# A planner's stage order and its scan density in a fused kernel of four vision layers

## What is computed

```python
# layers 0, 2, 3 (each of 8 images, 56*56 pixels, 128 channels in 4 groups, 9 points)
xp = x @ w_in + b_in
h = gelu(batch_norm(depthwise_conv3x3(x)))
offset, mask = h @ w_off + b_off, softmax(h @ w_msk + b_msk)
y = sum over 9 points of mask * bilinear_sample(xp, point + offset)   # 4 corners a point
x = x + gamma1 * layer_norm(y @ w_out + b_out)
x = x + gamma2 * layer_norm(gelu(x @ w_fc1 + b_fc1) @ w_fc2 + b_fc2)
# layer 1 (Di = 256 channels, N = 16 states, K = 4 directions, L = 3136)
xb = silu(depthwise_conv3x3(layer_norm(x) @ in_proj))
h = h * exp(dt_t * A) + (dt_t * u_t) * B_t      # a recurrence over L, for each k, d, n
y_t = sum over n of h * C_t
x = x + (layer_norm(y) * silu(z)) @ out_proj;  x = x + mlp(layer_norm(x))
```

## The kernel before, in words

| drain at the end of stage | next stage | rounds (full scan ticks among them) at 2.611 | at 2.656 | at 12 |
|---|---|---|---|---|
| 16, (0, 7) | (2, 5) | 23 (4) | 3 (3) | 0 |
| 20, (2, 6) | (3, 6) | 51 (51) | 53 (53) | 42 |
| 21, (3, 6) | (2, 7) | 4 (0) | 0 | 0 |
| 22, (2, 7) | (3, 7) | 42 (0) | 42 (0) | 42 |
| 23, the end | none | 22 (0) | 22 (0) | 22 |

## Time and profile before

### The profile page before, as it was taken

One profiled execution on the slowest core, in us unless ns is written; L12 is line 12 of the kernel. 1 busy time (PEld: TensorE's weight loads), 2 busy tenths in 40 slices (PEclk: granted clock), 3 DMA queues, 4 the chain that ended last, 5 costly groups with the idle time before them and its releaser, 6 DMA issues.

```text
span 30032.1 us, 287320 instructions
## 1 busy us (share of the span) xinstructions
PE 22752.8 (76%) x94224; PEld 14355.0 (48%) x94224; DVE 22824.8 (76%) x36140; ACT 12178.8 (41%) x21705; POOL 21870.4 (73%) x21172
## 2 busy tenths in 40 slices
PE   5588788787887888877887788777877787777444
PEld 4444455444554454444544454445544454445433
DVE  1289987989599868998788859997799968994212
ACT  1144444444444444444444435444444444443000
POOL 6777777777677777777677767776677767566767
PEclk7798889888888888888988888888888888888666
DMA  3212222221222222212222122212222222112221
GB/s 76 74 54 68 55 68 68 61 65 52 75 63 56 64 74 54 66 52 62 70 62 66 49 73 59 61 54 66 60 59 64 55 71 55 46 49 70 63 58 53
DMA packets 2410663, 1854.55 MB, mean 62 GB/s; under 512 B 1686547, under 2 KB 2045509, under 8 KB 2409165
## 3 DMA queue, kind: packets, MB, share of 16 engines
q0 software_dynamic: 677376, 1388.62, 17.3%
q1 hardware_dynamic: 1731788, 447.55, 6.7%
HBM read 1569.35 MB, written 265.21 MB: 61 GB/s over the span
## 4 chain that ended last, share of the span: by engine, by line
DVE 35%; PE 29%; POOL 14%; issue 12%; ACT 7%; DMA 1%; SPq 1%; DVEq 0%; ACTq 0%; POOLq 0%
POOL d_g L746 14%; DVE l_wk L1334 7%; DVE l_wk L1311 7%; PE d_p L1037 6%; PE l_acc L1019 5%; DVE l_wk L1328 5%; DVE d_g L1354 5%; PE d_pr L1185 3%; DVE l_wk L1313 2%; PE d_pr L1239 2%; ACT l_pm L797 2%; PE d_pr L1072 1%; PE d_pr L1051 1%; ACT L973 1%; PE d_pr L1232 1%
## 5 line engine op out<-in xcount | busy, mean ns | idle before, releaser
L746 POOL DMA_INDIRECT d_g<-table,d_idx x21168 | 21870.2, 1033 | 8119.0 <-issue 6395.7
L1037 PE MATMUL d_p<-d_g,c_ident 128*128 128x128 f32 x43200 | 6019.1, 303 | 2046.9 <-DVE d_g L1354 2043.0
L1019 PE MATMUL l_acc<-l_wk,c_ident 128*128 128x448 f32 x14336 | 7290.6, 638 | 331.5 <-DVE l_yx L1299 263.7
L1037 PEld LDWEIGHTS d_p<-d_g,c_ident 128*128 128x128 f32 x43200 | 5874.6, 218 | 3118.9 <-DVE d_g L1354 2149.0
L1324 DVE TENSOR_TENSOR l_wk<-l_wk,l_pb 128x896 f32<-128x896 f32 x3584 | 3814.9, 1064 | 1604.7 <-PE l_pb L988 1601.3
L797 ACT ACTIVATE l_pm<-l_wk,l_a 128x448 f32<-128x448 f32 x3584 | 2271.2, 634 | 6232.1 <-DVE l_wk L1311 6219.5
L1019 PEld LDWEIGHTS l_acc<-l_wk,c_ident 128*128 128x128 f32 x14336 | 3174.7, 223 | 2397.9 <-issue 2224.1
L1334 DVE TENSOR_TENSOR l_wk<-l_wk,l_pc 128x896 f32<-128x896 f32 x3584 | 3795.0, 1059 | 38.0 <-ACT l_carry L778 24.2
L1311 DVE TENSOR_TENSOR_SCAN l_wk<-l_pm,l_carry,l_wk 128x448 f32<-128x448 f32 x3072 | 3496.9, 1138 | 5.1 <-ACT l_pm L797 2.3
L1354 DVE TENSOR_TENSOR d_g<-d_g,d_wt 128x512 f32<-128x512 f32 x1281 | 812.6, 688 | 2291.6 <-DMA d_g<-table,d_idx 2291.3
L1328 DVE TENSOR_TENSOR_SCAN l_wk<-l_wk 128x224 f32<-128x224 f32 x3584 | 2421.3, 676 | 0.3
(11 more groups left out here) (180 smaller groups left out, 23765.5 us busy)
## 6 DMA issues: line engine op xcount, KB each, us to landing
d_g<-table,d_idx POOLq DMA_INDIRECT x21168
table<-d_pst SPq DMA_DIRECT2D x2376, 64.0 KB
hd<-d_hst SPq DMA_DIRECT2D x168, 224.0 KB
d_htc<-hd SPq DMA_DIRECT2D x144, 256.0 KB
d_xin<-mid SPq DMA_DIRECT2D x112, 224.0 KB
mid<-d_xo SPq DMA_DIRECT2D x192, 128.0 KB
d_xres<-mid SPq DMA_DIRECT2D x192, 128.0 KB
d_xin<-in_x SPq DMA_DIRECT2D x56, 224.0 KB
```

Source lines behind the costliest of these rows:

```text
L746: e.indirect_dma_start(out=m.g[Q % SLOTS][:, j, :], out_offset=None, in_=m.table[k % 2], in_offset=bass.IndirectOffsetOnAxis(ap=m.idx[G % ...
L1019: ins = e.matmul(m.acc[:, h, 0:448], m.ident[:, :], m.hb[x % 4][:, h, :], start=(n == 0), stop=(n == 15))
L1037: ins = e.matmul(m.p0[:, t % 2 * 128:t % 2 * 128 + 32 * w], m.ident[:, :], m.g[Q % SLOTS][:, w * p:w * p + w, 32 * r:32 * r + 32], start=( ...
```

## The change

Two places of the code are touched. In `stage_order` the stages (0, 6) and (3, 0) swap places (8 and 9), and so do (3, 6) and (2, 7) (21 and 22): the order then ends with (2, 6), (2, 7), (3, 6), (3, 7). In `schedule` the bisection allows no forced round beyond those that pace 12 has. No instruction of any engine is added or taken away by either: they are put in another order.

```diff
-        return [(0, 0), (0, 1), (0, 2), (0, 3), (0, 4), (2, 0), (0, 5), (2, 1), (3, 0), (0, 6), (2, 2), (3, 1), (2, 3),
-                (3, 2), (3, 3), (2, 4), (0, 7), (2, 5), (3, 4), (3, 5), (2, 6), (3, 6), (2, 7), (3, 7)]
+        return [(0, 0), (0, 1), (0, 2), (0, 3), (0, 4), (2, 0), (0, 5), (2, 1), (0, 6), (3, 0), (2, 2), (3, 1), (2, 3),
+                (3, 2), (3, 3), (2, 4), (0, 7), (2, 5), (3, 4), (3, 5), (2, 6), (2, 7), (3, 6), (3, 7)]
...
     free = Planner(n, high).forced
     for _ in range(10):
         mid = (low + high) / 2
-        if Planner(n, mid).forced <= free + 40:
+        if Planner(n, mid).forced <= free:
             high = mid
```

## The result

The changed kernel takes 30255.07 us (median of 4 runs, 30238.17 to 30270.23), against 30014.83 us for the kernel before, measured beside it (30010.79 to 30018.79). The ratio is 1.008 [1.0062, 1.0097]: slower by 240 us, where 690 us were forecast. The profiled execution took 30238.17 us, with a span of 30236.2 us and a mean granted clock of 0.845 (0.846 before). So its span is 204 us longer than that of before (30032.1 us), and this is the difference to take apart.

The account below looks back on a forecast made before the run. DVE's list was taken to bound the kernel while scans run, POOL without scans. - 349 + 1239 - 100 - 100 = + 690 us on 30034.1 us, less 16 us to the median, gave 30710 us; range 30000 to 31300 us (0.80).

Parts of the forecast that it names:

- The sign: Whole kernel: the change makes it slower, chance 0.81.
- DVE in the scan phase: While scans run: ticks cost DVE the same in all, 83 thirds fewer beside them at 4.2 us save 349 us.
- the upper bound of 5.8 us: Scan phase: most a third beside scans might cost, letting about 1.6 us of mixed-stage DVE idle time go with it.
- The pace: Scan ticks: pace rises from 2.611 to about 2.80, layer 1 ends at third 1538, 83 thirds earlier.
- The tail: After the scans: 83 more thirds where POOL alone sets the pace, at 14.93 us each, + 1239 us.
- A third beside scans: Scan phase: each third no longer beside scan ticks saves 4.2 us, bounds 3.13 and 5.8 us.
- The two drains beside scans: Before stages 21 and 17: removing them gains 100 us, not POOL's waits of 341.1 and 176.6 us; bounds 60 and 135.
- POOL is the bound throughout: Rival, whole kernel: POOL sets the time, its removed waits count in full, faster at 29440 or 29335 us; chance 0.12.
- Waits for B shrink: Rival, full and mixed stages: denser ticks halve DVE's waits, 500 to 700 us come back, 30000 to 30250 us; chance 0.10.
- The pace lands higher: Rival, scan ticks: at pace 2.95 they end 157 thirds earlier, + 1485 us, 31500 us; chance 0.08.

Follow-up runs that it names:

- e6_slack: Kernel before at its own pace 2.611, with layer 2 of images 1 to 4 a stage later in the order: 29860.75 us, ratio 0.9943.
- e8d_denser_apart: Changed kernel's order at pace 2.95, next stage's preparation held out of the transitions: 31039.28 us, 1.0334 of the kernel before.
- e1: Kernel before with the strict limit on forced rounds alone, order unchanged: 0.9832, 0.9871 and 0.9856 of the kernel before on three chips with standstills.
- e7_slack_apart: Kernel before at pace 2.611, layer 2 of images 1 to 4 a stage later, preparation held out of transitions: 29799.36 us, ratio 0.9926.
- e4b_before_apart: Kernel before at its own pace 2.611 and order, next stage's preparation held out of the transitions: 29806.19 us, ratio 0.9928.

## Why the prediction was wrong, and where it was right

**The sign was right, the size three times too large.** The step that failed is "DVE in the scan phase", in its first words: "The ticks cost it the same in all". I had read a full stage, found DVE's list full, and let that stand for the whole stretch of ticks. In the 3.5 ms of transitions PE sets the time, not DVE's list. Of the 337 us by which DVE idles in stage 19, 291 lie in the transition from 23983 to 24456 us (473 less 182.25). I had seen the idle time, and let a part of it go with the thirds (in the upper bound of 5.8 us), rather than ask which engine held the stage up and with what. The pace moves 89 preparation steps out of that regime, and with them PE's waits for inputs just written: a term of the sum that was missing altogether.

By the table above, the missing term is -535 us, and what it gave back beside the full ticks shows in the smaller saving there, -346 instead of -449. The two are -432 us of the -487 us between forecast and trace; the rest is the tail (-43) and the start (-12). At the 3.7 us a step that `e6_slack` measured, the 89 steps are 329 us; the other 100 of the 432 us are not shown to be the steps' alone, and 43 of them are the eighth transition's.

**The parts, one by one.**
- The pace: 2.802 and end third 1539, forecast 2.80 and 1538. Line 1479 ended at 26.71 ms, not 27.15, by what the transitions lost. It still lies in stage 20. Full stages took 1275 and 1292 us, not 1240 to 1280.
- The tail: 83 thirds at 14.98 us are 1243 us, less 147 for what went with them. Forecast +1139, measured +1096. Besides the 105.2 us before stage 23, POOL had waited 49.0 us for indices before stage 22, where the 4 rounds after stage 21 lie. In the changed kernel it waits for no indices after the scans. The prediction gave this second wait nothing, and it is about the 43 us by which the tail was missed. The tail is what makes the kernel slower.
- A third beside scans: 346 us for 74 thirds fewer there, 4.7 us with the drain before stage 21 in it and 3.3 with 100 us for the drains taken off, forecast 4.2. That it lies so near is luck: the 89 steps came in there, and at 2 us each (an estimate) the thirds and the drain saved 524 us, 7 us a third. The next 64 saved about 1 us each by the same reckoning (`e8d_denser_apart`). So there is no one price of a third.
- The two drains beside scans: POOL's 341.1 and 176.6 us went away, and the stretch of full ticks, which holds the longer of them, got shorter by 346 us with the thirds' saving in it. So they did not count in full beside the thirds. The 100 us given to them were not measured apart.
- *POOL is the bound throughout* fell: POOL's waits for buffers rose by 485 us and full stages by 70 to 90 us.
- *Waits for B shrink* named nearly the right time (30000 to 30250 us; the span is 30236), and the wrong cause. The waits for B did not shrink, 1601.3 before and 1640.2 us after. Its observation, that in mixed stages something would come back, is the one that was true.
- *The pace lands higher* did not happen; made to, at 2.95, it costs 3.3% (31039 us), where this rival had 31500.

**What stays open.** The two edits could not be priced apart on a chip of the first kind: `e1` fell on chips with standstills three times. From the plans alone, the limit gives the pace (2.802 in either order) and the order takes away the 84 rounds of drains (106 to 22). The exchange in the middle, (0, 6) and (3, 0), does nothing to the pace, the end third or the steps in transitions of the list; it was not run by itself. The changed kernel was not run on a chip with standstills. Its neighbours with 24 and 120 steps in transitions are 1.4 to 2.2% faster than before there, so it may be too; that is argued. The cause of the standstills is open as well.

## What to carry to other kernels

Work that is laid in between other work has a price by the regime it lands in: the same preparation step cost 4 to 6 us in a stretch mostly bound by TensorE, the more where its input had only just been written, and 2 beside scans bound by VectorE. Before a pace or an order is changed, list for each regime which engine is full in it, and what the planner's rules will carry from the one to the other. And a version found this way, the old pace with the steps kept out of the transitions (`e7_slack_apart`, `e4b_before_apart`), is 0.7% faster than the kernel before, with the same work in another order.

## What the runs showed of the hardware

The same program takes 30.0 ms on one chip and 35.1 to 35.3 ms on three others, at a granted clock of 0.79 instead of 0.845, and the sign of a change of 1% can differ between them: the strict limit and the higher pace were 1.3 to 2.2% faster than before on those three, while the higher pace was 0.8% slower on the first. A comparison holds for the chips on which it was made. And a chunk of 224 KB that is read back from DRAM, by a transfer issued 2.3 to 4.2 us after that of its write, kept TensorE waiting 4.5 us on average (31.7 us in 7 waits, in the transition of before from 23983 to 24456 us).
